# Decoder kernel: the low halves of one token half's expert activations are subtracted on GpSimd, and the steps stand in a new order

## The reference: what is computed

```python
gate_probs = softmax(xf @ gate_w.T)
topk_scores, topk_idx = top_k(gate_probs, 2)          # renormalised to sum 1 -> combine
h = relu(einsum('td,ehd->teh', xf, w1) + b1)          # 8 experts, hidden 512
out = einsum('ted,te->td', einsum('teh,edh->ted', h, w2) + b2, combine)
```

## Time and profile before

| what | value |
| --- | --- |
| runs | 411.15 us median, 411.04 to 412.64 |
| span of the profiled execution | 406.8 us |
| PE busy | 329.0 us, 81% |
| DVE busy | 301.8 us, 74% |
| ACT busy | 229.3 us, 56% |
| POOL busy | 85.7 us, 21% |

### The profile page before, as it was taken

How to read it: one execution, slowest core, us unless ns; L and a number is a source line. 1 busy time by engine, 2 the same in 40 slices (tenths; PEclk the granted TensorE clock), 3 DMA queues, 4 the chain that set the end, 5 groups by cost and what they waited for, 6 DMA issues and landing times. The chain is left out here.

```text
span 406.8 us, 8723 instructions
## 1 busy us (share of the span) xinstructions
PE 329.0 (81%) x3144; PEld 228.1 (56%) x3144; DVE 301.8 (74%) x788; ACT 229.3 (56%) x376; POOL 85.7 (21%) x170
## 2 busy tenths in 40 slices
PE   1547898789977985676889986697799999989993
PEld 1445566456766764552556662464366667677773
DVE  6898536878886867999665699989960887866664
ACT  1438885656525243250834652467187786778881
POOL 5835877522024004000300210220000010100000
PEclk9988999998998956779998798999999999999999
DMA  7910000000041040000000000000000000000000
GB/s 207 419 68 2 2 2 2 2 2 0 2 150 60 10 197 1 0 2 0 2 2 0 2 2 0 1 3 0 1 2 3 1 2 2 2 27 2 2 2 26
DMA packets 4187, 12.32 MB, mean 30 GB/s; under 512 B 490, under 2 KB 2802, under 8 KB 3122
## 3 DMA queue, kind: packets, MB, share of 16 engines
q1 hardware_dynamic: 4146, 11.77, 8.0%
HBM read 11.24 MB, written 0.52 MB: 29 GB/s over the span
## 5 line engine op out<-in xcount | busy, mean ns | idle before, releaser
L914 ACT ACTIVATE region_p<-double 128x1024 f32<-128x1024 f32 x64 | 63.9, 1029 | 16.8 <-PE double L1466 4.9
L1376 DVE TENSOR_TENSOR tmp<-hid,tmp 128x1024 f16<-128x1024 f32 x32 | 39.2, 1225 | 26.6 <-ACT tmp L1003 26.2
L764 POOL TENSOR_SCALAR rstd<-mv 128x2 f32<-128x2 f32 x24 | 7.4, 307 | 221.3 <-DVE mv L1063 220.5
L993 ACT ACTIVATE hid<-double,b1s 128x512 f32<-128x512 f32 x64 | 40.4, 682 | 21.1 <-PE double L1723 20.9
L1736 PE MATMUL single<-w,tmp 128*128 128x128 f16 x720 | 42.6, 219 | 2.3 <-issue 2.3
L1736 PEld LDWEIGHTS single<-w,tmp 128*128 128x128 f16 x720 | 41.1, 98 | 5.5 <-issue 3.3
L1723 PE MATMUL double<-xnT,w 128*128 128x512 f16 x168 | 39.2, 379 | 0.5 <-DVE mx L1217 0.4
L1003 ACT ACTIVATE tmp<-hid 128x1024 f16<-128x1024 f32 x32 | 33.2, 1057 | 1.3 <-ACT hid L993 0.4
L1071 DVE TENSOR_SCALAR xn<-x,mv,rstd 128x128 f32<-128x128 f32 x64 | 23.0, 457 | 12.8 <-POOL rstd L770 6.9
L1217 DVE TENSOR_REDUCE mx<-double 128x4 f32<-128x1024 f32 (+1 forms) x24 | 29.4, 1223 | 0.8
L1445 PE MATMUL double<-qT,region_k 128*128 128x256 f16 x128 | 22.5, 286 | 9.0 <-DVE region_k L1108 5.5
(11 more groups left out here) (279 smaller groups left out, 732.5 us busy)
## 6 DMA issues: line engine op xcount, KB each, us to landing
w<-in_w1a SPq DMA_DIRECT2D x2, 1024.0 KB, 10.8
w<-in_w2a SPq DMA_DIRECT2D x2, 1024.0 KB, 12.4
w<-in_w1b SPq DMA_DIRECT2D x2, 1024.0 KB, 5.2
w<-in_w2b SPq DMA_DIRECT2D x2, 1024.0 KB, 7.3
row<-in_row SPq DMA_DIRECT2D x1, 800.0 KB, 7.2
wb<-in_wb SPq DMA_DIRECT2D x1, 709.0 KB, 8.4
x<-in_x SPq DMA_DIRECT2D x4, 128.0 KB, 2.9
out<-x SPq DMA_DIRECT2D x4, 128.0 KB, 1.9
```

The costliest lines, as they stand in the source:

```text
L914: a.activation(probs[:, slot("prob", key), :], psum(step), ACT.Exp, scale=SCALE).then_inc(psum_done[PSUM.slot(step)], 1)
L993: a.activation(hid0[:, slot("hid0", (h, e, n)), cols], psum(step)[:, cols], ACT.Relu, bias=b1s[:, c:c + 1]).then_inc(psum_done[PSUM.slot(s ...
L1376: then(v.tensor_tensor(hid[:, 1].rearrange("p c n -> p (c n)"), hid0[:, slot("hid0", (h, e, n)), :], hid[:, 0].rearrange("p c n -> p (c n) ...
```

## The change

The planner's cost of `hs` names POOL with 2.3 us instead of DVE with 1.1 us where h = 0. The DVE instruction of `hs` is left out for h = 0, and the same subtraction with the same operands stands in POOL's program. The semaphore `hidden_low` becomes two, one for each half; whoever waited for it waits for the one of its half. All three planner constants and the whole table `AHEAD` are replaced, so that the order of all 553 steps is planned anew. No transfer, no matmul, no other instruction is added or removed.

```diff
-            add(("hs", h, e, q), [("mup", h, e, q)], ("A", 1.0), ("D", 1.1),
+            add(("hs", h, e, q), [("mup", h, e, q)], ("A", 1.0), ("D", 1.1) if h else ("G", 2.3),
                 behind=[q and ("hs", h, e, 0)])
...
-NARROW, BANKS, PREFER = 2, 4, 0.12
+NARROW, BANKS, PREFER = 2, 4, 5.31471839468948e-16
...
-PULL, SWITCH = 0.00095, 0
+PULL, SWITCH = 2.64824293125011e-05, 0
...
-AHEAD = {"casts": (3.8, 0), "fdown": (-5.1, -3.8), "fup": (0, -1.9), "ga": (0.2, -1.2),
-         "gb": (-0.2, 3), "gc": (0.1, -0.7), "gd": (-0.9, 0), "hs": (0.4, 35.2), "k4": (0.9, 0),
...
+AHEAD = {"casts": (47.4, 20.8), "fdown": (0.2, -1.7), "fup": (-0.2, 0.1), "ga": (0.2, -1.7),
+         "gb": (55.6, 23), "gc": (-1, 0.1), "gd": (-0.3, -0.9), "hs": (0.1, 17), "k4": (3.4, 0),
...
-                eng.wait_ge(sem("hidden_low"), count(("hs",), last))
+                low_written(eng, last)
+
+        def low_written(eng, step):
+
+            n = sum(1 for s in ORDER[:INDEX[step] + 1] if s[0] == "hs" and s[1] == step[1])
+            eng.wait_ge(sem(f"hidden_low{step[1]}"), n)
...
+                elif kind == "hs" and step[1] == 0:
+
+                    _, h, e, n = step
+                    pool.wait_ge(sem("hidden_high"), count(("hs",), step))
+                    hid = hid1[:, slot("hidden", (h, e)), :, 2 * n:2 * n + 2, :]
+                    then(g.tensor_tensor(hid[:, 1].rearrange("p c n -> p (c n)"),
+                                         hid0[:, slot("hid0", (h, e, n)), :],
+                                         hid[:, 0].rearrange("p c n -> p (c n)"), ALU.subtract),
+                         "hidden_low0")
...
-                elif kind == "hs":
+                elif kind == "hs" and step[1] == 1:
...
-                         "hidden_low", wait=False)
+                         "hidden_low1", wait=False)
...
                     pe.wait_ge(sem("hidden_high"), count(("hs",), ("hs", h, e, 1)))
-                    pe.wait_ge(sem("hidden_low"), count(("hs",), ("hs", h, e, 1)))
+                    low_written(pe, ("hs", h, e, 1))
```

More of the change, by code:

```diff
@@ L467, in the_order @@
     return order, at, max(ends.values())
-NARROW, BANKS, PREFER = 2, 4, 0.12
-PULL, SWITCH = 0.00095, 0
-AHEAD = {"casts": (3.8, 0), "fdown": (-5.1, -3.8), "fup": (0, -1.9), "ga": (0.2, -1.2),
[7 rows of a table removed]
-         "mxe5": (-1, -0.4), "mxs": (-2.5, 0.7), "nxa": (-5.4, -0.7), "nxb": (-4.9, -1.6),
[6 rows of a table removed]
-         "qkv": (-1.7, 0), "ropea": (5.8, 0.1), "ropeb": (1.7, 0), "rows": (60.3, -0.9),
[5 rows of a table removed]
+NARROW, BANKS, PREFER = 2, 4, 5.31471839468948e-16
+PULL, SWITCH = 2.64824293125011e-05, 0
+AHEAD = {"casts": (47.4, 20.8), "fdown": (0.2, -1.7), "fup": (-0.2, 0.1), "ga": (0.2, -1.7),
+         "gb": (55.6, 23), "gc": (-1, 0.1), "gd": (-0.3, -0.9), "hs": (0.1, 17), "k4": (3.4, 0),
+         "kck": (-0.4, -0.4), "kct": (-0.7, -0.7), "kcv": (-1.4, -1.4), "lna0": (345.5, 344.7),
[5 rows of a table added]
+         "mxe5": (0.4, 59.4), "mxs": (-0.6, 13.6), "nxa": (-0.6, -0.6), "nxb": (-1.1, -2.9),
[13 rows of a table added]
 ORDER, AT, ABOUT = the_order()
```

## The result

The changed kernel's median is 416.98 us (414.51 to 422.01, 4 runs) against 411.1: a ratio of 1.0122 [1.0075, 1.0169], 1.2% slower. The forecast was 405.2 us, faster by 1.4%, with a range up to 416.0; the result lies outside it. The profiled execution took 417.02 us with a span of 415.3. Medians in this document are over all runs of a kernel, while ratios and their intervals leave out the runs that lie more than 1.5% above the fastest of the same kernel (here the one of 422.01).

What follows compares the result with a forecast made beforehand. From 281 to 357 us it took DVE to bound 15 us, PE 46, a mixed chain 15. Span 406.8 - 2.45 + 1.0 - 2.5 - 3.0 + 1.0 = 400.85; median 411.15 - 5.95 = 405.2 us, range 396.5 to 416.0.

Steps and rivals of the forecast that it cites:

- What POOL takes: One 128x1024 subtraction on POOL: 2.2 us, from a line through smaller instructions, bounds 1.2 to 2.7.
- Parts 1 and 2: 281 to 357 us: two subtractions leave the DVE-bound stretch, gain 2.45 us; the other fourteen lose 1.0 us.
- product waits: Rival at PE's down products in half 0: they wait for POOL's longer subtraction; 416.5 us, chance 0.14.
- Part 3b: Before 260 us: the new order mixes PE-bound and DVE-bound stretches; gain 3.0 us, bounds 5 lost to 7.5 gained.
- Part 3a: 260 to 296 us: one more expert's PE work fills PE idle time; gain 2.5 us, bounds 0 to 7.0.
- Part 4: 281 to 357 us: DVE instructions wait for POOL; loss 1.0 us on the path, bounds 0 and 4.
- lock: Rival: every POOL subtraction holds up one DVE instruction for 1.1 us; 414.3 us, chance 0.11.

Runs made afterwards that it cites:

- g3: All low halves on DVE; the changed kernel's order up to the first expert product, the old order after it: 0.8% faster than the kernel before.
- e2: The changed kernel's new order with all low-half subtractions on DVE as before: 412.7 us, ratio 1.006 to the kernel before.
- e3: The changed kernel with each POOL subtraction cut into four of 256 columns: 407.57 us, ratio 0.9865 to the kernel before.
- h4: Repeat of e3, the changed kernel with four pieces per POOL subtraction: 408.42 us, ratio 0.9865 to the kernel before.
- h1: The changed kernel, whole subtractions on POOL, with the gate transposes and their products of sequences 1 and 3 moved later: 416.77 us.
- h2: h1 (gate transposes moved later) with each POOL subtraction in four pieces: 412.46 us.
- k1: The changed kernel with each POOL subtraction cut into eight of 128 columns: slower than four pieces; no time given.
- f4: e2 plus an unused POOL subtraction, reading constants, behind each activation of half 0: 14.6 us over e2.
- f5: e2 plus an unused, write-only POOL memset of 1.8 us behind each activation of half 0: ratio 1.0022.
- g1: The changed kernel with half 0's subtractions of experts 5 and 7 whole on DVE, the other twelve on POOL in four pieces: 412.87 us.
- k2: g3 with the low halves of experts 0 to 3 of half 0 on POOL in four pieces: gains nothing on g3.
- e1: The kernel before, its old order kept, with all 16 subtractions of half 0 whole on POOL: 411.4 us, ratio 1.0015.
- f3: e1 (old order) with each POOL subtraction in four pieces: 418.4 us.

## Why the prediction was wrong

- **What POOL takes.** Right: 2.2 us taken, 2.128 measured.
- **Parts 1 and 2.** Two subtractions left the DVE-bound stretch as said, but 1.9 of the 2.45 us came back at once, since the sum of the maxima, 0.16 to 0.2 us like its neighbours, took 2.08 beside POOL. The wait of a product for POOL (part 2, and the rival "product waits") did not come: PE waits for POOL nowhere between 280 and 380 us, ACT 0.4 us. That rival's time, 416.5, was hit by another mechanism, which is luck.
- **Part 3b**, the term I called weakest, was right in size: 3.0 us taken. The experts start 3.3 us sooner in the profiled execution and 3.9 in the mean of all profiles, and g3 has 0.8%. It was a guess within bounds, so the size is partly luck.
- **Part 3a failed.** No expert moved into the stretch. Its third expert product starts 17.8 us after the first (290.6 and 272.8), before it was 18.3 (294.4 and 276.1). The idle that I let it fill stayed: PE has 21.29 of 27.2 us from 272.8 to 300 in the changed kernel, and 21.30 of the same length from 276.1 before. An expert's product needs the wide bank, and the maxima hold the banks; I named that and priced it at 1.6 us. The late part of the new order lost time even on DVE (a middle of 83.3 us in e2 against 77.3, up to 2.1 of it the weight splits), and this I had not allowed for at all: my lower bound for this term was 0.
- **Part 4 failed**, and with it the sum. I had the mechanism from the earlier trace rows, spread it evenly (half of 2.2 us, for a dozen groups) and put 1.0 us of it on the path. The place decides, not the mean. The gate instructions, of 0.1 to 0.3 us each, which I did not count since they cost nothing before, form serial chains for which PE waits, and two of these chains met two whole subtractions each. With the order fixed, POOL costs 416.3 or 417.0 less 412.7, 3.6 to 4.3 us by the medians and 2.1 to 2.5 by the ratios, whose intervals overlap: 2 to 4 us where I had 1.0. By the table of parts it is 1.5 us in the middle and 2.7 behind it.
- **The clock** was in no term. Behind each PE wait of 3 to 4 us the profile of the changed kernel shows some 5 us at a granted clock of 0.54 and 0.50 (338.2 to 343 us and 357.6 to 363), which is the lower of its two levels, 1.2 GHz: six products take 2.74 us for 1.46. The same 3144 matmuls keep PE busy for 329.0 us before, 329.7 in e3, 333.1 in e2 and 334.7 in the changed kernel. By these single executions most of it (4.1 of 5.7 us) comes with the new order and without POOL, and with the pieces it is nearly gone. The longest wait does not tell the clock: it is 2.3 us in e2 and in e3, at 0.92 and 1.00. From e2 to the changed kernel PE's waits grow by 3.6 us and its busy time by 1.6; that is an estimate of how the hold's cost divides, from one execution each.
- **The rival "lock"** had the mechanism and 414.3 us, too little by 2 to 3, and I gave it 0.11. Its price of 2.2 us on the path left out the gate chains and the clock. What spoke against it in my text, that the maxima read PSUM, is true and beside the point: the chain is late by the small instructions between the large ones.
- **The range.** By my own bounds on the parts the sum reaches 421.0 us (411.15 - 1.2 + 2 + 0 + 5 + 4). The 399 to 410 that I gave as the forecast's own range is narrower than that, and so is the end of the stated range, 416.0.
- **The offset.** I set the median against the span with 4.35 us between them. The profiled execution itself took 408.6 us, 1.8 over its span, so 2.5 of the 4.35 was spread between runs; it does not change the sign.

Shown: in the new order the length of POOL's instructions costs time, since with nothing else changed four pieces take the ratio from 1.0111 and 1.0122 to 0.9865 (e3, h4; h1 to h2 likewise), up to a point (k1). Reading instructions on POOL alone cost time (f4), writing ones cost nothing clear (f5). Moving the gate transposes does not help (h1). The new order costs 0.6% with no subtraction on POOL at all (e2). Argued only: that the two met chains account for the whole cost of POOL, and that POOL and the new order make each other worse rather than add up. Open: why gains do not add (g1, k2), and what in the late part of the new order costs e2 its 6 us beyond the weight splits and a granted clock of 0.83 in three of its windows (280 to 290, 340 to 350, 350 to 360 us).

The best version is e3: a ratio of 0.9865 to the kernel before in both comparisons, with medians over all runs of 407.57 and 408.42 us.

## What to carry to other kernels

Before elementwise work goes to POOL, list the small SBUF-to-SBUF instructions of DVE that stand in a serial chain before PE: here each was lengthened by up to a whole POOL instruction, whatever its size. If the work must go there, cut it so that one piece is short against the slack of that chain, but count the added latency for whoever waits for the last piece. And price a step's order and its engine together: here the same four pieces made the old order 1.6% slower than whole subtractions (e1 to f3) and the new one 2.5% faster (changed kernel to e3).

## What the runs showed of the hardware that was not expected

- DVE instructions on 2 and on 8 elements per partition took 2.10 and 2.04 us beside POOL subtractions of 2.13 and 2.12 us.
- Two-input work on DVE lengthened POOL's as well: 2703 ns on average in f4 against 2128 for the changed kernel's subtraction of the same shape.
- A POOL memset of 1.8 us left DVE's two-input subtractions at 1226 ns (f5).
- POOL's subtraction cost 456, 695, 1176 and 2128 ns for 128, 256, 512 and 1024 columns, so cutting it in four cost 31% more of POOL's time and made the kernel 2.3% faster (416.98 to 407.57).
